# Attention and mixture-of-experts block: four consecutive tokens in each partition, and both expert results of a token fetched together

## What is computed

```
h = layer_norm(x, ln1_w, ln1_b)
q, k, v = h @ Wq, h @ Wk, h @ Wv                      # per head, 32 channels
wei = softmax(where(causal, q @ k.T * C ** -0.5, -1e30))
x = x + concat_heads(wei @ v) @ Wo + bo
nx = layer_norm(x, ln2_w, ln2_b)
noisy = nx @ Wr + br + noise * softplus(nx @ Wn + bn)
router_out = softmax(noisy where among its top 2, else -1e30)
expert_out = sum over e of router_out[..., e] * (relu(nx @ W1[e] + b1[e]) @ W2[e] + b2[e])
final = where(sigmoid(nx @ Wsk + bsk) <= 0.5, x + expert_out, x)
```

## Time and profile before

| what | value |
|---|---|
| median of 3 runs | 845.84 us (844.49 to 845.9) |
| time of the profiled execution | 843.46 us |
| span of its trace | 841.5 us |
| PE / DVE / ACT / POOL busy | 608.7 / 590.0 / 490.1 / 411.0 us |
| combination stage, from its first DVE instruction to the end of the span | 753.92 to 841.5 us |
| packets moved by the DMA engines | 164172, 127.32 MB |

### The profile page before, as it was taken

The page is one execution under the profiler, slowest core; times in us unless marked ns, Lnnn a source line. Parts: engine busy times, 40 slices in busy tenths (PEclk is TensorE's granted clock), DMA queues, the critical chain, the costliest instruction groups (busy, mean ns, idle before and its releaser), DMA issues.

```text
span 841.5 us, 32036 instructions
## 1 busy us (share of the span) xinstructions
PE 608.7 (72%) x11268; PEld 467.6 (56%) x11268; DVE 590.0 (70%) x2270; ACT 490.1 (58%) x979; POOL 411.0 (49%) x479
## 2 busy tenths in 40 slices
PE   0578889989989898898987215999999999710000
PEld 0356766766667676675756213777777777600000
DVE  3366777777787777877766553788777788527887
ACT  2448576776776767667665414888888888500000
POOL 3000756666565756666564770466666666530000
PEclk9889999999999999998978656999999999855555
DMA  9763231322313223131743437676677776239997
GB/s 93 230 192 101 66 96 56 94 63 89 94 56 92 64 86 94 59 93 59 145 123 93 148 122 268 206 234 228 226 231 240 243 242 236 74 104 293 298 295 227
DMA packets 164172, 127.32 MB, mean 151 GB/s; under 512 B 38050, under 2 KB 142595, under 8 KB 164128
## 3 DMA queue, kind: packets, MB, share of 16 engines
q1 hardware_dynamic: 127264, 90.00, 36.4%
q10 hardware_dynamic: 24576, 20.98, 8.5%
q0 software_dynamic: 12288, 15.77, 5.9%
HBM read 73.86 MB, written 62.78 MB: 162 GB/s over the span
## 4 chain that ended last, share of the span: by engine, by line
PE 49%; ACT 12%; DVE 12%; issue 11%; DMA 7%; ACTq 3%; POOL 2%; DVEq 1%; SPq 1%; POOLq 0%
PE ps L505 7%; DMA out<-z 5%; PE ps L529 5%; ACT z L682 4%; PE ps L542 4%; PE ps L545 3%; PE ps L632 3%; PE ps L554 3%; PE ps L633 3%; PE ps L634 3%; PE ps L644 3%; PE ps L645 3%; PE ps L646 3%; PE ps L512 2%; PE ps L603 2%
## 5 line engine op out<-in xcount | busy, mean ns | idle before, releaser
L1131 POOL DMA_INDIRECT expert_rows<-pay,rows_of x256 | 253.7, 991 | 226.6 <-ACT pay L759 81.5
L1143 POOL DMA_INDIRECT expert_results<-z,words x128 | 136.1, 1063 | 105.7 <-DVE z L1023 74.4
L1037 DVE TENSOR_TENSOR hlo<-h,hhi 128x512 fp32r<-128x512 f32 x128 | 89.8, 702 | 45.6 <-ACT hhi L793 43.9
L791 ACT ACTIVATE h<-ps,w1x 128x512 f32<-128x512 f32 x128 | 88.2, 689 | 35.1 <-PE ps L634 30.8
L682 ACT ACTIVATE z<-xres,shift,rstd 128x128 f32 (+1 forms) x256 | 102.0, 482 | 1.8 <-DVE shift L855 1.5
L793 ACT ACTIVATE hhi<-ps,w1x 128x512 fp32r<-128x512 f32 x128 | 87.1, 681 | 0.0
L542 PE MATMUL ps<-hT,wq 128*128 128x512 f32 x64 | 48.8, 855 | 42.7 <-ACT hT L714 42.7
L698 ACT ACTIVATE log_var<-var_eps 128x8 f32<-128x8 f32 (+1 forms) x36 | 7.5, 208 | 112.0 <-DVE var_eps L844 87.6
L554 PEld LDWEIGHTS ps<-pT,v_sb 32*32 32x32 f32 x4096 | 44.5, 107 | 46.5 <-issue 44.6
L529 PE MATMUL ps<-kT,qT 32*32 32x32 f32 x4096 | 58.0, 200 | 6.3 <-issue 1.8
L644 PE MATMUL ps<-hhi,w2x 128*128 128x512 f32 x128 | 56.8, 444 | 4.2 <-issue 4.2
(11 more groups left out here) (150 smaller groups left out, 1402.5 us busy)
## 6 DMA issues: line engine op xcount, KB each, us to landing
w1x<-split_weights SPq DMA_DIRECT2D x33, 514.0 KB
w2x<-split_weights SPq DMA_DIRECT2D x33, 512.5 KB, 4.7
expert_results<-zeros SPq DMA_DIRECT2D x32, 512.0 KB
pay<-expert_rows SPq DMA_DIRECT2D x33, 264.0 KB, 3.5
xres<-in_r_x SPq DMA_DIRECT2D x32, 256.0 KB, 2.9
split_weights<-w2x ACTq DMA_DIRECT2D x16, 512.0 KB
hhi<-expert_results SPq DMA_DIRECT2D x32, 256.0 KB, 3.8
hlo<-expert_results SPq DMA_DIRECT2D x32, 256.0 KB, 3.9
```

The lines of the kernel that those rows point to most:

```text
L791: nc.scalar.activation(h32[:, c % 2], ps[:, c, :], ACT.Relu, bias=b1_c).then_inc(s_h32_made, 1)
L1037: ev.tensor_tensor(hlo[:, c], h32[:, c % 2], hhi[:, c].bitcast(F32), ALU.subtract).then_inc(s_h_lo, 1)
L1131: g.indirect_dma_start(rows, bass.IndirectOffsetOnAxis(ap=rows_of[:, odd, k * J + j:k * J + j + 1], axis=0), pay[:, odd, k, j, :], None, b ...
L1143: g.indirect_dma_start(results, bass.IndirectOffsetOnAxis(ap=words[:, slot, j:j + 1], axis=0), yrow[slot][:, j, :], None, bounds_check=K * ...
```

## The change

Partition p of group n now holds the four consecutive tokens `n*512 + 4p + j`, j = 0 to 3. In DRAM these are one run of 2 KB of x and of the output, where before each tile's row was a run of 512 B; the noise of a partition's four tokens is a run of 128 B where it was 32 B. The result table is ordered by token and then choice, so the eight results of a partition's four tokens are one run of 4 KB, and one DMA in place of two brings them in.

The attention still works on batches of 32 consecutive tokens, so the order is turned on the way in and on the way out. On the way in, ACT's write of `hT` goes to every fourth element: column `4p + j` for partition p of tile j. On the way out, the matmuls of L554 write their 32 columns to PSUM with a step of 32 elements between consecutive columns of each four, and ACT's copy to `oT` moves runs of 8 elements.

```
-    xt = x.rearrange("b t c -> (b t) c").rearrange("(n p) c -> p n c", p=P)
-    noise_t = noise.rearrange("b t e -> (b t) e").rearrange("(n p) e -> p n e", p=P)
-    out_t = out.rearrange("b t c -> (b t) c").rearrange("(n p) c -> p n c", p=P)
+    x_rows = x.rearrange("b t c -> (b t) c")
+    noise_t = noise.rearrange("b t e -> (b t) e").rearrange("(n p j) e -> p n (j e)", p=P, j=J)
+    out_rows = out.rearrange("b t c -> (b t) c")
-    results_t = results.rearrange("(k n p) c -> p k n c", k=K, p=P)
...
-        yin = [y.rearrange("p k (j c) -> p k j c", c=C).bitcast(F32) for y in yin]
+        yin = [y.rearrange("p k (j c) -> p (k j) c", c=C).bitcast(F32) for y in yin]
...
+        def group(a, n):
+            return a[bass.ds(n * G, G), :].rearrange("(p j) c -> p j c", j=J)
...
-                sp.dma_start(tiles(xres, n), xt[:, bass.ds(n * J, J), :]).then_inc(x_in[par], 16)
+                sp.dma_start(tiles(xres, n), group(x_rows, n)).then_inc(x_in[par], 16)
...
-            sp.dma_start(noise_sb[:], noise_t).then_inc(s_noise_in, 16)
+            sp.dma_start(noise_sb[:].rearrange("p (n j) e -> p n (j e)", j=J), noise_t).then_inc(s_noise_in, 16)
...
-                for k in range(K):
-                    sp.dma_start(yin[slot][:, k], results_t[:, k, bass.ds(n * J, J), :]).then_inc(f_in[slot], 16)
+                sp.dma_start(yin[slot], results[bass.ds(n * K * G, K * G), :].rearrange("(p r) c -> p r c", p=P)
+                             ).then_inc(f_in[slot], 16)
...
-                                m = nc.tensor.matmul(ps[h * HS:(h + 1) * HS, b, P + j * T:P + (j + 1) * T],
+                                to = ps[h * HS:(h + 1) * HS, b, P:2 * P]
+                                to = to.rearrange("s (q m i) -> s m i q", q=J, m=J)[:, j]
+                                m = nc.tensor.matmul(to,
                                                      v_sb[b * T:(b + 1) * T, odd, j, h * HS:(h + 1) * HS],
                                                      pT[b * T:(b + 1) * T, odd, h, j, :], start=True, stop=True,
...
-                        m = nc.tensor.matmul(ps[:, 4, j * P:(j + 1) * P], oT[:, j].rearrange("c b t -> c (b t)"),
+                        m = nc.tensor.matmul(ps[:, 4, j * P:(j + 1) * P], oT[:, j],
...
-                    nc.scalar.activation(hT[:], ps[:, 4, :], ACT.Identity, bias=norm1[:, 1:2],
+                    nc.scalar.activation(hT[:].rearrange("c (p j) -> c j p", j=J),
+                                         ps[:, 4, :].rearrange("c (j p) -> c j p", j=J), ACT.Identity, bias=norm1[:, 1:2],
                                          scale=norm1[:, 0:1]).then_inc(s_hT_made, 1)
...
-                    nc.scalar.activation(oT[:], ps[:, 0:NB, P:2 * P].rearrange("c b (j t) -> c j b t", t=T),
+                    to = oT[:].rearrange("c j (m b i) -> c b (j m) i", m=J, b=NB)
+                    nc.scalar.activation(to, ps[:, 0:NB, P:2 * P].rearrange("c b (r i) -> c b r i", i=T // J),
                                          ACT.Copy).then_inc(s_oT_made, 1)
...
-                act.dma_start(out_t[:, bass.ds(n * J, J), :], fin[:, par]).then_inc(f_out[par], 16)
+                act.dma_start(group(out_rows, n), fin[:, par]).then_inc(f_out[par], 16)
...
-                dve.wait_ge(f_in[slot], quad(n, slot, 16 * K) + 16 * K)
+                dve.wait_ge(f_in[slot], quad(n, slot, 16) + 16)
...
-            g.iota(token[:], [[N, K], [P, J]], base=0, channel_multiplier=1,
+            g.iota(token[:], [[1, K], [K, J]], base=0, channel_multiplier=K * J,
```

More of the change, by code:

```diff
@@ L133, in build @@
         pT = sb("pT", [P, 2, H, J, T])
-        oT = sb("oT", [C, J, NB, T])
+        oT = sb("oT", [C, J, P])
         nT = sb("nT", [C, G])
@@ L1053, in combine @@
                 par = slot % 2
-                dve.wait_ge(f_in[slot], quad(n, slot, 16 * K) + 16 * K)
+                dve.wait_ge(f_in[slot], quad(n, slot, 16) + 16)
                 for j in range(J):
-                    m = ev.scalar_tensor_tensor(half[:, par, j:j + 1], yin[slot][:, 0, j:j + 1],
+                    m = ev.scalar_tensor_tensor(half[:, par, j:j + 1], yin[slot][:, K * j:K * j + 1],
                                                 tile(gates, n, j)[:, 0, 0:1], tile(xres, n, j), ALU.mult, ALU.add)
@@ L1061, in combine @@
                 for j in range(J):
-                    m = ev.scalar_tensor_tensor(fin[:, par, j:j + 1], yin[slot][:, 1, j:j + 1],
+                    m = ev.scalar_tensor_tensor(fin[:, par, j:j + 1], yin[slot][:, K * j + 1:K * j + 2],
                                                 tile(gates, n, j)[:, 0, 1:2], half[:, par, j:j + 1], ALU.mult, ALU.add)
@@ L1125, in step @@
                     apart(pool, (s_word_made, n + 1))
-                    g.tensor_scalar(token[:], token[:], float(G), None, ALU.add).then_inc(s_token_next, 1)
+                    g.tensor_scalar(token[:], token[:], float(K * G), None, ALU.add).then_inc(s_token_next, 1)
                     apart(pool, (s_route, n * ROUTE + ROUTE),
```

## The result

The changed kernel takes 862.86 us in the median of 4 runs (861.23 to 864.28), against 845.87 us for the kernel before on the same chip. The ratio is 1.0212, with a 95% interval of 1.0179 to 1.0244: slower by about 17 us, clear of the noise. The span of the profiled execution is 862.0 us, 20.5 us more than before.

What follows compares the result with a forecast made beforehand. It took the chain through `hT` to bound attention, and DMA and store landings the combination stage. From 845.84 us, -6.6 (combination), -1.0 (start) and +12.8 (`hT` write) made +5.2, so 851.0 us, range 836 to 862.

Steps and rivals of the forecast that it cites:

- The chain through `hT`, paid 32 times: Attention stage: `hT` lies on the chain of waits in every pass, so its extra cost is paid for all 32 groups.
- The write's price, 12.8 us in all: Attention stage: ACT's strided write of `hT` costs 0.40 us more a pass, times 32; range 0 to 15 us.
- the upper of the two bounds: ACT's write of `hT`: a halved rate adds 0.48 us; the other bound above was 0.35 us.
- The clock: Attention stage, rival: more passes at PE's lower clock, or a dearer step, giving 856 to 866 us; chance 0.14.
- ten more: Attention stage, within a rival of chance 0.14: ten more passes fall to the lower clock, each adding about 1 us.
- The combination stage, -6.6 us: Combination stage: longer runs end the DMA bandwidth limit and stores land sooner, saving 6.6 us; range 0 to 9.
- the bound with no gain: Combination stage, rival: store landings do not shorten, at 3.95 us nothing is gained, 2.65 us per group stay, 857.6 us; chance 0.10.
- The start, -1.0 us: Kernel start: the noise load in a quarter of the runs lets the last bias land earlier, saving 1.0 us; range 0 to 2.
- L554 and `oT` as free: Attention stage: L554's strided PSUM writes and `oT` in runs of 8 cost 0; rival, L554 slows, +6 us, chance 0.04.
- The argument from the low-clock pass: L554: 128 matmuls took 1.35 us at clock 0.86, 1.55 at 0.50, so half-rate writes cost at most 0.20 us a pass.

Runs made afterwards that it cites:

- e1: The changed kernel with `hT` written contiguously again, attention working on a group's tokens in another order: 841.62 us, ratio 1.0001.
- e2: The kernel before with only the strided write of `hT` added, tokens in another order: 863.79 us, ratio 1.0287.
- e8: The kernel before with four buffers for the stored tile in place of two: 836.55 us, ratio 0.9923.
- e10: e3 with each combination-stage load bringing only the first 2 KB of each partition's 4 KB, other results left out: 833.49 us, ratio 0.9884.
- e3: The changed kernel with the turn moved from ACT's write to PE's transposes, writing PSUM with a 16 B step: 840.33 us, ratio 0.999.
- e4: The changed kernel with the turn in ACT's read of PSUM, step 512 B, and `hT` written in order: 839.37 us, ratio 0.999.
- e9: The kernel before with 6 added matmuls on constant data in PE's wait for `hT`: 833.15 us, ratio 0.9903.
- e5: The changed kernel, strided write kept, with 8 added matmuls on constant data in PE's wait for `hT`: 841.51 us, ratio 0.9989.
- e7: e3 with four buffers for the stored tile in place of two: 829.56 us, ratio 0.9846.

## Why the prediction was wrong

The direction was right and the time was not: 862.86 us lies just above the range of 836 to 862 and 12 us above the 851 forecast. By the prediction's own steps:

- **The chain through `hT`, paid 32 times: right.** e1 and e2 show it from both sides.
- **The write's price, 12.8 us in all: about right in size.** `hT` grew by 0.48 us, the upper of the two bounds, but ACT's next activation started only 0.37 us later; with the clock held it cost 9.7 us. The Trainium skill, Vector Engine (DVE) Microarchitecture Reference, section Measured stream behaviour on trn2, has 1.71 to about 2.5 ns a column for such destinations against 1.054, measured on DVE; the estimate from it was 0.34 to 0.74 us a pass. ACT's write, (1250 - 774) / 512 = 0.93 ns an element or 0.48 us a pass more, lies within it.
- **The clock: the first step that failed.** The sum took it as 0 and kept it as a rival, "ten more" passes at about 1 us, with a chance of 0.14. It came, with 10.0 us, and the nearness to ten passes at 1 us is in part luck: slow q's became only 3 more, and the rest is that the clock stayed down longer, up to 3.1 us in a pass. The rows for it were there: the kernel before already ran 15 of its 32 q's slowly after PE's wait, so lengthening that wait was likely to cost more. A term with a known sign had no place at zero.
- **The combination stage, -6.6 us: the second that failed, +1.0 measured.** The landing of a store was put between 2.9 us, that of an x load, and 3.6. It was 3.9: the bound with no gain, kept as a rival with 0.10, came true. The sum had an error of its own. It gave a landing of 3.6 us 2.47 us a group and booked 5.7 us of gain for it, but 3.6 was already the median of the kernel before, whose groups take 2.65; that case held no gain. DVE waited there in 16 of 32 groups, for up to 1.7 us, behind the stores that came late, and a median does not show those. The share of 0.98 was read as bandwidth; e8 shows 323 GB/s through the same short runs. The x load, with 2.9 us, runs in a stage with a DMA share of 0.30 and was no measure for a store here; e10 gives 3.0 us only when half of the loads' bytes are gone. What makes a landing of 3.6 us into one of 3.9 with longer runs stays open.
- **The start, -1.0 us: failed, 0 measured.** The noise load halved its time and the bias behind which DVE waits landed at the same moment.
- **L554 and `oT` as free: right.** The argument from the low-clock pass held. The Trainium skill, PSUM — Partial Sum Buffer, section Specifications (TRN2), says that an access that is not contiguous slows matmuls significantly; here neither L554 (206 ns before, 203 to 211 after) nor the transposes of e3 with a step of 16 B (286 ns against 297) did, and the measurements decide.

Account of the span: +9.7 for the write, +10.0 for the clock, +1.0 for the combination stage, -0.3 behind it, 20.4 of 20.5 us. Against the forecast's +5.2: the clock is 10.0 of the difference, the combination stage 7.6, the start 1.0, and the write gave 3.1 back. By the means over all traces the clock's part is some 2 us larger and the write's smaller by less than one; the order of the steps is the same.

## What to carry to other kernels

When an order has to be turned between two engines, put the step into a PSUM access, PE's write or ACT's read, and keep ACT's write to SBUF in runs: here the first two were free (e3, e4) and the last cost 480 ns for 512 single elements. A wait that grows on a chain in front of PE has two prices, its own length and the clock; look at how often the clock already falls behind that wait, and fill it if there is work that harms nothing. Before giving transfers longer runs, find out whether the stage waits for bandwidth or for a landing: here a busy share of 0.98 did not tell, and two more buffers gained 0.8 to 1.5% where four times longer runs gained nothing that could be measured.

## What the runs showed of the hardware

- ACT's write of single elements 16 B apart costs 0.93 ns an element more (1250 against 774 ns for 512); in runs of 8 elements nothing (594 against 592). ACT's read from PSUM with a step of 512 B costs nothing (773 ns).
- PE's writes to PSUM with steps of 16 B (286 ns a transpose against 297) and of 128 B (203 to 211 against 206 ns) cost nothing.
- 6 to 8 short matmuls in a wait of 0.9 to 1.4 us kept the granted clock at 1.00 over a stage where it had been 0.94 and 0.89, and gave back 8.7 and 18.7 us from the first q to the last (e9, e5).
- Stores of 256 KB landed in 3.0 us beside 256 KB of loads a group (e10); beside 512 KB in 3.6 to 4.1 us in runs of 512 B and in 3.8 to 4.3 us in runs of 2 KB. DMA engines moved 323 GB/s in runs of 512 B (e8) and 322 in long ones (e7), with DVE as the bound in both.
